# A Mamba block between two expert FFNs on one core: products with B made with time on the partitions, and the FFN on sorted pairs of token and expert

## The reference

```python
x = x + 0.5 * ffn(layernorm(x))
x = x + attn(layernorm(x))
x = x + 0.5 * ffn(layernorm(x))

def ffn(x):                      # 8 experts, hidden size 512, the best 2 for each token
    probs = softmax(x @ gate_w)
    vals, idx = top_k(probs, 2); vals = vals / sum(vals)
    combine = zeros(N, 8) with vals at idx
    for e in range(8):
        out += combine[:, e:e+1] * (silu(x @ w1s[e]) @ w2s[e])

def mamba(x):                    # inner size 256, 16 states
    xm, res = split(x @ in_w.T + in_b)
    xm = silu(causal_conv4(xm) + conv_b)
    dt, B, C = split(xm @ xp_w.T)           # 64, 16, 16
    delta = softplus(dt @ dt_w.T + dt_b)
    for t: h = h * exp(delta[t] * A) + (delta[t] * xm[t])[:, None] * B[t][None, :]
           y[t] = h @ C[t]
    return ((y + xm * D) * silu(res)) @ out_w.T + out_b

def attn(x):
    x1 = x + mamba(rmsnorm(x)); out2 = mamba(rmsnorm(x1))
    return x1 + memory_attend(out2)         # chunked linear attention with decay
```

## Time and profile before

| | |
|---|---|
| median of 3 runs | 1802.31 us (1799.83 to 1803.46) |
| the profiled execution's own time | 1800.41 us |
| its span, first to last instruction | 1798.6 us |
| mean granted clock of TensorE | 0.902 |
| busy: VectorE / TensorE / ScalarE / GpSimd | 1584.7 / 1464.6 / 1102.3 / 310.3 us |
| DMA: bytes moved, mean rate | 131.93 MB, 73 GB/s |

### The profile page before, as it was taken

The page is one execution under the profiler, slowest core; times in us unless marked ns, Lnnn a source line. Parts: engine busy times, 40 slices in busy tenths (PEclk is TensorE's granted clock), DMA queues, the critical chain, the costliest instruction groups (busy, mean ns, idle before and its releaser), DMA issues. The chain is left out here.

```text
span 1798.6 us, 26309 instructions
## 1 busy us (share of the span) xinstructions
PE 1464.6 (81%) x8672; PEld 1256.5 (70%) x8672; DVE 1584.7 (88%) x2421; ACT 1102.3 (61%) x2173; POOL 310.3 (17%) x366
## 2 busy tenths in 40 slices
PE   5878656988989888988889888888889888558868
PEld 4667545877778677777778677776778677447757
DVE  5259998999999999999999999999999999999821
ACT  2266545756766666756766677756776676448422
POOL 0001231122112211122112121122112121111100
PEclk9989767998999899998999899998999899569869
DMA  5014434433443334433443344443443344443400
GB/s 198 1 24 79 80 71 82 88 73 59 81 84 72 70 71 90 87 72 59 79 88 62 74 77 90 81 77 58 76 82 73 67 77 89 82 82 72 93 7 7
DMA packets 43947, 131.93 MB, mean 73 GB/s; under 512 B 3984, under 2 KB 12176, under 8 KB 43664
## 3 DMA queue, kind: packets, MB, share of 16 engines
q0 software_dynamic: 32256, 117.45, 34.4%
q1 hardware_dynamic: 11536, 12.56, 2.2%
HBM read 10.46 MB, written 2.10 MB: 7 GB/s over the span
## 5 line engine op out<-in xcount | busy, mean ns | idle before, releaser
L926 DVE TENSOR_TENSOR_SCAN hs<-dA,dbu 128x1024 f32<-128x1024 f32 x256 | 583.9, 2286 | 5.2 <-issue 3.7
L574 ACT ACTIVATE raw<-b_h 128x512 f32<-128x512 f32 x512 | 305.9, 598 | 320.9 <-PE b_h L326 306.5
L635 ACT ACTIVATE dA<-delta,A 128x255 f32<-128x255 f32 x1024 | 421.6, 495 | 14.8 <-DVE delta L899 8.3
L1114 POOL DMA_DIRECT2D acc<-G x224 | 195.2, 872 | 1026.5 <-DVE G L938 583.0
L403 PE MATMUL b_r<-bcr,selr 128*128 128x256 f32 x1024 | 242.6, 332 | 139.0 <-DVE G L938 71.6
L916 DVE TENSOR_TENSOR dbu<-du,b_r 128x1024 f32<-128x1024 f32 x256 | 305.8, 1205 | 7.8 <-issue 4.1
L324 PE MATMUL b_h<-xh,w1h 128*128 128x512 f32 x512 | 245.3, 479 | 78.1 <-DVE ob L852 29.2
L403 PEld LDWEIGHTS b_r<-bcr,selr 128*128 128x128 f32 x1024 | 176.2, 205 | 180.3 <-DVE G L938 80.8
L938 DVE TENSOR_TENSOR G<-hs,b_r 128x1024 f32<-128x1024 f32 x224 | 271.6, 1213 | 8.2 <-issue 5.0
L333 PE MATMUL b_out<-w2s,raw 128*128 128x128 f32 x2048 | 252.2, 275 | 0.0
L333 PE MATMUL b_h<-w2s,raw 128*128 128x128 f32 x2048 | 250.2, 275 | 0.0
(11 more groups left out here) (137 smaller groups left out, 1425.7 us busy)
## 6 DMA issues: line engine op xcount, KB each, us to landing
acc<-G POOLq DMA_DIRECT2D x224, 512.0 KB, 4.5
xin<-x_dram SPq DMA_DIRECT2D x8, 256.0 KB, 2.8
raw<-w_dram SPq DMA_DIRECT2D x1, 2048.0 KB, 11.2
out_dram<-ob SPq DMA_DIRECT2D x8, 256.0 KB, 3.2
prm<-pack_dram SPq DMA_DIRECT2D x1, 1124.5 KB, 5.2
hs<-sel_dram SPq DMA_DIRECT2D x2, 512.0 KB, 12.4
G<-sel_dram SPq DMA_DIRECT2D x2, 512.0 KB, 7.5
dA<-early_dram SPq DMA_DIRECT2D x1, 512.0 KB, 11.6
```

The source lines that it names most:

```text
L574: do(hT[e % 2][:, c, :], H[i % 2][:, :], ACT.Silu).then_inc(f_hact, 1)
L635: last = do(dA[j % 4][:, d, k, 1:], delta[b][:, k, 1:], ACT.Exp, scale=A[:, k, s:s + 1])
L926: V.tensor_tensor_scan(flat(hs[j % 2]), flat(dA[j % 4]), flat(dbu[j % 2]), 0.0, ALU.mult, ALU.add)\
L1114: Q.dma_start(acc[b][:, :, :, :].rearrange("p d h t -> p (d h t)"), G[j % NG][:, :, :, :].rearrange("p d h t -> p (d h t)"), accum_op=ALU. ...
```

## The change

**Products with B.** `dbu` is no longer made by VectorE. In the head of a pass, TensorE turns du (`du_turn`, four transposes) so that time is on the partitions, and ScalarE takes it to `duT` (`du_turned`). B is made with time on the partitions too: four small products more in `x_proj`; it lies behind dt in `dtT`. Now B of a state is one value per partition, and GpSimd makes the products: `scale`, four tensor-scalars of 128 x 256 per round (`c3` to `c7` in the pass, `h0` to `h2` in the pass before), into one of four buffers `scaled`. TensorE turns them back into PSUM, four transposes per state (`scan_input`, `t0` to `t15`), into one of two banks. The scan is now one per state (512 elements), with dbu read from PSUM; `t` of a state waits for the scan two before. The C rows (`k0` to `k7`) have one bank and wait for G of the round before. G and the accumulating DMAs stay.

**FFN on sorted pairs.** Each token goes only to its two experts. The 1024 pairs of token and expert are sorted by expert, each expert's part padded to tiles of 128: 15 tiles. VectorE and TensorE find the place of each pair (`ffn_count`, `ffn_place`), GpSimd scatters the normed tokens to DRAM by 8 indirect DMAs (`sc`), SyncE loads them in five chunks of three tiles and the w1 of each tile's expert (256 KB) into one of four buffers, its number read from `eid` into a register. TensorE turns a chunk (`T`), and for each tile makes up (`U`, four fp32 products of 128 columns) and down (`D`, the same, w2 chosen by a register); ScalarE takes each out of PSUM (`F`). SyncE stores the results by chunks, GpSimd gathers both results of a token by 8 indirect DMAs (`ga`), and VectorE adds them once (`ffn_sum`, 8 instructions per FFN). The splits into high and low parts go. Steps of the routing are done a half-group earlier (for the next FFN, `nx`).

All orders are written anew, and the loop over groups 1 to 5 is written out. On GpSimd some drains become waits on semaphores.

The diff, cut to its core (of `ORDER` the new strings of pass 1):

```diff
...
+NSC = 4
+AHEAD = 3
+CH = 3
+NT = 2 * TOK // P + E - 1
+CHUNKS = NT // CH
+NW = 4
+NH = 3
...
+    yield "T", 0
+    for i in range(NT):
+        yield "U", i
+        if i % CH == 0 and i // CH + 1 < CHUNKS:
+            yield "T", i // CH + 1
+        if i:
+            yield "D", i - 1
+    yield "D", NT - 1
...
 ORDER = {
     "tensor": (
...
+        "t0 p1 t1 p2 t2 k0 p1 t3 t4 p3 fturn p1 fgate k1 t5 t6 p3 fcount p3 k2 p2 t7 p1 k3 out t8 p5 turn t9 t10 "
+        "k4 in t11 t12 k5 t13 xp k6 dt t14 k7 t15 dx",
...
+        "d0 F6 F7 d1 F8 F9 d2 d3 F10 F11 F12 F13 F14 fxT d4 F15 F16 F17 F18 F19 d5 d6 F20 ftanh F21 F22 F23 F24 "
+        "turned r xm d7 proj sp dx",
...
     "vector": (
...
+        "s0 s1 s2 fstats g0 fnorm s3 s4 g1 flog ftop fplace s5 gate g2 s6 s7 xsum g3 s8 un s9 g4 s10 s11 g5 s12 "
+        "s13 fweights g6 low s14 delta s15 g7 fsum",
...
     "gpsimd": (
...
+        "froot c3 c4 c5 c6 a1 sc0 sc1 sc2 sc3 a2 c7 fkeep rms sc4 a3 sc5 sc6 sc7 a4 ga0 ga1 ga2 ga3 a5 ga4 ga5 "
+        "ga6 ga7 a6 h0 a7 h1 h2 rs",
...
+            def chunk_in(n, c):
+                sp.wait_ge(s_scat, 16 * 2 * TILES * (n + 1))
+                wait(sp, f_hmm, (n - 1) * ITEMS + RING_OF["T", c] + 1)
+                sp.dma_start(xsort[:, c * CH:(c + 1) * CH, :], rows(xs_d[n % 2], c)).then_inc(s_xs[c], 16)
+            def expert_in(n, i):
+                k = n * NT + i
+                sp.wait_ge(f_tile, n + 1)
+                if k >= NW:
+                    m, j = divmod(k - NW, NT)
+                    sp.wait_ge(f_hmm, m * ITEMS + RING_OF["U", j] + 1)
+                e = sp.value_load(eid[n % 2][0:1, i:i + 1], min_val=0, max_val=E - 1)
+                sp.dma_start(wst[k % NW][:, :], w1[e]).then_inc(s_w[k % NW], 16)
+            def chunk_out(n, c):
+                wait(sp, s_gat, 16 * 2 * TILES * (n - 1))
+                sp.wait_ge(f_ys, n * CHUNKS + c + 1)
+                sp.dma_start(rows(ys_d[n % 2], c), ys[:, c * CH:(c + 1) * CH, :]).then_inc(s_ys[c], 16)
...
+            def ffn_up(n, i):
+                r, k, t = RING_OF["U", i], n * NT + i, i % CH * P
+                pe.wait_ge(s_w[k % NW], 16 * (k // NW + 1))
+                wait(pe, f_hact, n * ITEMS + max(r - 1, RING_OF["T", i // CH] + 1))
                 for c in range(HC):
-                    last = mm(EOUT[e % 2][:, j * D:(j + 1) * D], hT[e % 2][:, c, j * P:(j + 1) * P],
-                              w2s[:, e, c, :], start=c == 0, stop=c == HC - 1)
-                if j == TILES - 1:
-                    last.then_inc(f_ymm, 1)
+                    w = slice(c * P, (c + 1) * P)
+                    last = mm(H[r % 2][:, w], wst[k % NW][:, w], xsT[i // CH % 2][:, t:t + P], start=True, stop=True)
+                last.then_inc(f_hmm, 1)
+            def ffn_down(n, i):
+                pe.wait_ge(f_hact, n * ITEMS + RING_OF["U", i] + 1)
+                if i % CH == 0:
+                    wait(pe, f_ys, n * CHUNKS + i // CH)
+                e = pe.value_load(eid[n % 2][0:1, i:i + 1], min_val=0, max_val=E - 1)
+                for c in range(HC):
+                    last = mm(Y[:, i % CH * D:(i % CH + 1) * D], hT[i % NH][:, c, :], w2s[:, e, c, :],
+                              start=c == 0, stop=c == HC - 1)
+                last.then_inc(f_ymm, 1)
...
+                for j in range(T // P):
+                    for k in range(HALVES):
+                        mm(W[0][:, T + j * DS:T + (j + 1) * DS], xm[b][:, k, j * P:(j + 1) * P],
+                           par("xp")[:, k * P:k * P + DS], start=k == 0, stop=k == HALVES - 1)
...
+            def du_turn(g, i):
                 q, b = 4 * g + i, i % 2
-                if t == 0:
+                pe.wait_ge(q_du, q + 1)
+                for j in range(T // P):
+                    for k in range(HALVES):
+                        last = nc.tensor.transpose(W[1][:, j * DI + k * P:j * DI + (k + 1) * P],
+                                                   du[b][:, k, j * P:(j + 1) * P], ident)
+                last.then_inc(q_dumm, 1)
+            def scan_input(g, i, s):
+                q, (j, d) = 4 * g + i, divmod(s, DP)
+                pe.wait_ge(q_sc, q * NP + j + 1)
+                wait(pe, q_scan, q * DS + s - 1)
+                for k in range(HALVES):
+                    for t in range(T // P):
+                        last = nc.tensor.transpose(DBU[d][:, k * T + t * P:k * T + (t + 1) * P],
+                                                   scaled[j % NSC][:, d, t, k * P:(k + 1) * P], ident)
+                last.then_inc(q_dbu, 1)
+            def spread(g, i, j):
+                q, b = 4 * g + i, i % 2
+                if j == 0:
                     pe.wait_ge(q_bc, q + 1)
-                ring = lambda i, t: (t + SHIFT[i]) % RING
-                if t >= RING:
-                    kind, j = SPREAD[t - RING]
-                    pe.wait_ge(q_G if kind else q_dbu, q * NP + j + 1)
-                else:
-                    kind, j = next(SPREAD[o] for o in range(2 * NP - RING, 2 * NP)
-                                   if ring((i - 1) % 4, o) == ring(i, t))
-                    if not isinstance(g, int) or q > 0:
-                        pe.wait_ge(q_G if kind else q_dbu, q * NP - NP + j + 1)
-                kind, j = SPREAD[t]
+                wait(pe, q_G, q * NP + j)
                 for d in range(DP):
-                    last = mm(R[ring(i, t)][:, d * T:(d + 1) * T], selr[:, kind * DS + DP * j + d, :], bcr[b][:, :],
-                              start=True, stop=True)
-                last.then_inc(q_C if kind else q_B, 1)
...
+            def ffn_leave(n, x):
+                kind, k = LEAVES[x]
+                if kind == "U":
+                    table(SILUS)
+                if kind == "Y":
+                    act.wait_ge(f_ymm, n * NT + (k + 1) * CH)
+                    if not n and not k:
+                        act.wait_ge(s_zero, 32)
+                    wait(act, s_ys[k], 16 * n)
+                    do(ys[:, k * CH:(k + 1) * CH, :], Y.rearrange("p (i d) -> p i d", d=D), ACT.Copy).then_inc(f_ys, 1)
+                    return
+                r = RING_OF[kind, k]
+                act.wait_ge(f_hmm, n * ITEMS + r + 1)
+                if kind == "T":
+                    do(xsT[k % 2][:, :], H[r % 2][:, 0:CH * P], ACT.Copy).then_inc(f_hact, 1)
+                else:
+                    wait(act, f_ymm, n * NT + k - NH + 1)
+                    do(hT[k % NH][:, :, :], H[r % 2][:, :].rearrange("p (c t) -> p c t", c=HC), ACT.Silu)\
+                        .then_inc(f_hact, 1)
...
+            def ffn_sum(f):
+                n, src, dst, g, is_first = f
+                dve.wait_ge(s_gat, 16 * 2 * TILES * (n + 1))
+                dve.wait_ge(f_weights, 2 * n + 2)
+                dve.wait_ge(f_keep, n + 1)
                 for k in range(2):
-                    V.tensor_tensor(hit[:, k, :, :], hit[:, k, :, :],
-                                    c01[:, k, :].unsqueeze(2).broadcast_to([P, TILES, E]), ALU.mult)
-                dve.drain()
-                V.tensor_tensor(comb[:, :, :], hit[:, 0, :, :], hit[:, 1, :, :], ALU.add)
-                dve.drain()
-            def ffn_sum(f, e):
-                n, src, dst, g, is_first = f
-                dve.wait_ge(f_ymm, n * E + e + 1)
-                wait(dve, f_yacc, n * E + e)
-                if e == 0:
-                    wait(dve, *((g_xam, g) if is_first else (s_store, g * 16)))
-                for j in range(TILES):
-                    last = V.scalar_tensor_tensor(
-                        out=dst[:, j, :], in0=EOUT[e % 2][:, j * D:(j + 1) * D],
-                        scalar=comb[:, j, e:e + 1], in1=(src if e == 0 else dst)[:, j, :],
-                        op0=ALU.mult, op1=ALU.add)
+                    for j in range(TILES):
+                        last = V.scalar_tensor_tensor(
+                            out=dst[:, j, :], in0=yk[:, k, j, :], scalar=c01[n % 2][:, k, j:j + 1], in1=dst[:, j, :],
+                            op0=ALU.mult, op1=ALU.add)
+                    if not k:
...
-            def scan_input(g, i, j):
-                q = 4 * g + i
-                dve.wait_ge(q_B, q * NP + j + 1)
-                wait(dve, q_scan, q * NP + j - 1)
-                V.tensor_tensor(dbu[j % 2][:, :, :, :],
-                                du[i % 2][:, :, :].unsqueeze(1).broadcast_to([P, DP, HALVES, T]),
-                                spread_rows(i, (0, j)), ALU.mult).then_inc(q_dbu, 1)
...
+            def scan(g, i, s):
+                q, (j, d) = 4 * g + i, divmod(s, DP)
                 dve.wait_ge(q_dA, q * NP + j + 1)
-                dve.wait_ge(q_dbu, q * NP + j + 1)
+                dve.wait_ge(q_dbu, q * DS + s + 1)
                 wait(dve, q_G, q * NP + j - 1)
-                V.tensor_tensor_scan(flat(hs[j % 2]), flat(dA[j % 4]), flat(dbu[j % 2]), 0.0, ALU.mult, ALU.add)\
-                    .then_inc(q_scan, 1)
```

(28 more changed lines are left out.)

560 lines of the change are left out of this document (338 added, 222 removed), and 39 rows, old and new, of the table ORDER.

## The result

Median of 4 runs 2011.61 us (2010.23 to 2016.05), before 1801.37 (1799.83 to 1803.46): ratio 1.118, 95% interval [1.116, 1.120]. The forecast was 1620, range 1530 to 1790, with 0.15 on slower. The profiled execution's span is 2008.6 us.

What follows compares the result with a forecast made beforehand. VectorE was taken as the bound, busy 1584.7 of 1798.6 us. The largest engine or chain per pass, mean 39.9 us, plus 10% coupling gave a pitch of 43.9; 31 steps plus 255 head and tail gave 1616, forecast 1620, range 1530 to 1790.

Steps and rivals of the forecast that it cites:

- With the fixed 0.19 of a two-element instruction I take 0.39: 12.5 us: GpSimd's products with B: 0.39 us for each of 32 per pass, 12.5 us, between bounds of 0.30 and 0.61.
- Wrong if a GpSimd product takes over 0.6 us: GpSimd's products with B: one of the stated conditions under which the forecast would be wrong.
- GpSimd is the bound: Rival, chance 0.12: indirect DMAs at 2.2 us make passes 1 and 3 61 and 58 us, pitch 50.3, 1818 us.
- I take zero, since each down piece follows an up piece: TensorE's register read of the expert's number in down pieces: no cost; from above 1.4 us per pass.
- The coupling, 10%: Waits between engines in each pass: 10% over the mean largest engine of 39.9 us, range 4 to 18%.
- Head and tail, 255: Time around the 31 steps from pass to pass: 255 us, from 251 before, plus 12, less 8.
- near 1830: Kernel's end if TensorE's transposes cost 275 ns apiece, 10.6 us more per pass; the forecast took 0.11 us instead.
- the 1818 of the falling clock: Rival, chance 0.10: transposes don't hold TensorE's clock, it falls to 0.70, pitch 50.3, 1818 us.
- the break-even clock: TensorE's granted clock at which the change gains nothing: 0.71, a pitch of 49.8 us.
- I set 2.0 us more per link: Accumulating DMAs: new transfers in the queues delay each of a pass's seven links by 2.0 us.
- tight coupling: Rival, chance 0.25: the orders of the engines fit, loss 4%, pitch 41.5, 1545 us.
- the chain of accumulations: Rival, chance 0.08: seven accumulating DMAs at 7.07 us set the pass, pitch 49.5, 1793 us.

Runs made afterwards that it cites:

- e3: The changed kernel with an addition of 0.0 as second operation in each GpSimd product with B, same result: 1793.97 us, ratio to before 0.9974.
- e7: e3 with the register read of each down piece's expert moved one piece earlier, behind the up piece, same result: 1757.8 us, ratio to before 0.9757.
- e17: e7 with half of each down product, half of each scan, the FFN's silu and all accumulating DMAs left out: 1615.8 us, ratio to before 0.8976.
- e14: e7 with two accumulators per pass, three links each, and two hT buffers instead of three, same result: 1777.1 us against 1757.8.
- e16: e7 with GpSimd's root before the last accumulation and its statistics at the head of VectorE's pass, same result: 1762.3 us, ratio to before 0.9799.
- e12: e7 with GpSimd's copy of the FFN's input put behind the scatters at both ends, same result: 1758.9 us against 1757.8.
- e1: Separate kernel without the model, timing series of eight single instructions: GpSimd multiplication alone 0.90 us, with a second operation 0.46.
- e13: e7 with all accumulating DMAs left out, a one-column memset signalling in their place: 1754.4 us against 1757.8.
- e4: The changed kernel with the four GpSimd products of a round made by one tensor-tensor of 1024 elements: 1881.1 us.
- e6: e3 with the expert's number a constant instead of a register read, so some tiles get the wrong w2: 1756.7 us.
- e10: e7 with two of the four products in each down piece left out: 1753.8 us against 1757.8.

## Why the prediction was wrong, step by step

**The step that failed: "With the fixed 0.19 of a two-element instruction I take 0.39: 12.5 us"** for GpSimd. The bounds, 0.30 and 0.61, came from xam, which multiplies and adds. I did not ask whether xam was of the same form. The trace before did show an instruction of GpSimd with one operation on 256 elements, the tensor-tensor `rs`, and I passed it over:

```profile
L1123 POOL TENSOR_TENSOR rs<-xam,x 128x256 f32<-128x256 f32 x16 | 25.9, 1618 | 0.0
```

Its shortest lasted 1.00 us. It reads two inputs, and some of its mean may be blocking beside VectorE, but as the nearest row by size and number of operations it belonged in the bounds: at 1.0 us apiece the products come to 32 us a pass. Measured: 0.94 us apiece in the kernel, 30.2 us a pass. With indirect DMAs, accumulations and the rest GpSimd was then busy 333.7 of 400 us in the middle, its waits for landings not counted. e3 shows what this step was worth: 214 us of the span, and the sign. "Wrong if a GpSimd product takes over 0.6 us" stood among the conditions. The rival "GpSimd is the bound" had the engine right and the cause wrong: indirect DMAs take 1.0 us, 1.3 apart with the idle time before each, near the 1.1 taken.

**The register read, "I take zero, since each down piece follows an up piece"**: 36 us (e3 to e7). Of e3's 109 stops 40 (31.5 us) come behind scan inputs, which wait for scans and often stand between the two pieces; but 22 (30.5 us) come directly behind an up piece. In the queue the read stood behind the down piece's wait for hT, and e7 moves it ahead of that wait too. Which of the two counted more was not told apart.

**The coupling, 10%.** With the two above put right the pitch is 47.45. The largest engine of each pass had a mean of 39.9 in the sum, so the loss is 19%, beyond the 18 of my range: 3.5 us by 31 steps, 110 us. (That mean stands: over the 31 steps of e7 it is 39.6. By engine, in its window from 600 to 1000 us, TensorE has 39.6 us a pass, 39.1 in the sum, at a clock of 0.94 where the sum took 0.9, so its work was set some 6% low; VectorE has 38.9 against 36.8, ScalarE 36.1 against 37.9, GpSimd, products at 0.49 us included, 31.2 against 33.7. That these errors cancel is luck.) The size of this term was wrong, and its reason at least in part: I raised the loss from 4% to 10% because four engines would be within 10% of each other. That explains why relieving one gives little, but the fifth of waits stays when one engine leads (e17). Which waits make it up is not settled; the ones that I moved in the passes (e14, e16) gave nothing.

**Head and tail, 255.** 287.9 in e7, 33 over: 13 in the tail, 20 in the head. In the tail 8 are the wait of GpSimd's copy for the store of the group before (e12), and some 3 the indirect DMAs, which stand 1.26 us apart (0.96 and 0.30 idle before each) where I took 1.1. The tail's other 2 and the head's 20 were not taken apart.

214 + 36 + 110 + 33 = 393, the whole of the miss (2008.6 - 1616). The first two are measured by edits; the last two are what is left between e7 and the sum, split at the pitch.

**Two faults of the working that did not decide.** The forecast has 10% of coupling, but "near 1830" (transposes at 275 ns) and the 1818 of the falling clock have none; with it they come to some 1995 and 1975 us, and the break-even clock to 0.78. And "I set 2.0 us more per link" went only into the rival, while the sum has the chain at 35.5 us.

**What held.** The scan of 512 elements from PSUM 1209 ns (1228). VectorE's work 1264.6 us in e3 (1229). Transposes 0.11 us apart: in e7 the four of a scan input take 0.60 us, the record of each 0.27. Table loads 236 (some 256), hidden. The products are not stretched beside the new scan (e1, L115). Queue 1 carries 18.1% of the span, 364 us of 16 engines (350), but a landing comes only 0.4 us later, not 2.0, and the chain is hidden (e13). **Rivals:** tight coupling fell, the chain of accumulations fell (e13, e14). The clock: mean 0.856 after, 0.87 to 0.93 in the four passes from 687 to 911 us, above the break-even of 0.71, and of 0.78 with the coupling. The Trainium skill (TensorE: Matmul & The Clock Gate, Part 4: PE-mode transpose) says that the fast clock does not engage for transposes; here, with transposes among products, it held at 0.94 (e7), so by this trace the rule does not reach this mixture.

## What to carry to other kernels

Price an instruction by a row of the same engine, shape and number of operations, and where there is none, measure it by itself before the work is moved to it. Moving work off a full engine pays only down to the next engine: add up each engine's pass first. The waits on top do not carry over from one schedule to the next: here they were 5% of the largest engine before and 14 to 23% in the new orders, whichever engine led, and no single cause was found. Here the change with two small edits (an addition of 0.0, the register read one piece earlier; e7) is 2.4% faster than the kernel before.

## What the hardware showed that I had not expected

- GpSimd's tensor-scalar with one operation takes 0.90 us for 128 x 256 fp32, with two 0.46; for 512 elements one takes 1563 ns, for 1024 2844. Why, the profile does not show.
- A GpSimd instruction stretches VectorE's xn (SBUF to SBUF) with its own length: median 340 ns before, 540 beside tensor-scalars of 0.49 us (e3), 1934 beside a tensor-tensor of 1.9 to 2.3 us (e4).
- Where TensorE reads a number of SBUF into a register, its weight loads stood idle 0.9 us on average (109 of 240 reads, e3); read behind the up piece and ahead of the wait for hT, it cost nothing (e7 against e6).
- With less work TensorE got a lower granted clock (0.94 to 0.91), and its busy time fell by 66 us where the records taken out are worth 108 at full clock (e10).
